# Two graph layers on one core: new order tables, fewer waits, and pair sums of the last group on GpSimd

## The reference

```python
def _L0_gnn_ref(item_embs, entity_embs, adj, W, a):
    scores = (Wh @ a1)[:, None] + (We @ a2)[None, :]
    e = jnp.where(scores > 0, scores, ALPHA * scores)      # ALPHA 0.2
    e = jnp.where(adj > 0, e, NEG_BIG)
    attention = jax.nn.softmax(e, axis=1)
    h_prime = attention @ entity_embs + item_embs
    return jax.nn.elu(h_prime)

def _L1_gnn_ref(x, adj_mat, U):
    deg = a.sum(axis=0)
    agg = jnp.einsum('ji,jd->id', a, x)
    return jax.nn.relu(agg @ U.T / deg[:, None])

h = jnp.maximum(_layernorm(x), 0.0)
x = x + _L0_gnn_ref(h, V, adj, W, a)
h = jnp.maximum(_layernorm(x), 0.0)
x = x + _L1_gnn_ref(h, adj, U)
```

## Time and profile before

| | us |
|---|---|
| median of 3 runs (415.91 to 420.17) | 417.25 |
| the profiled execution, its time | 417.24 |
| its span in the trace | 415.3 |
| PE busy | 347.2 (84%) |
| DVE busy | 298.0 (72%) |
| ACT busy | 275.2 (66%) |
| POOL busy | 115.0 (28%) |
| guards L828, 66 | 152.1 |
| scores L881, 41 | 49.3 |
| pair adds L890, 16 | 19.2 |

### The profile page before, as it was taken

One profiled execution on the slowest core, in us unless ns is written; L12 is line 12 of the kernel. 1 busy time (PEld: TensorE's weight loads), 2 busy tenths in 40 slices (PEclk: granted clock), 3 DMA queues, 4 the chain that ended last, 5 costly groups with the idle time before them and its releaser, 6 DMA issues.

```text
span 415.3 us, 17291 instructions
## 1 busy us (share of the span) xinstructions
PE 347.2 (84%) x7920; PEld 224.4 (54%) x7920; DVE 298.0 (72%) x423; ACT 275.2 (66%) x339; POOL 115.0 (28%) x120
## 2 busy tenths in 40 slices
PE   1737778298889797798899988899989899999996
PEld 0723555264456455454455434344534457999996
DVE  8799899457996568759984799965978683307333
ACT  2404789489998679779979999999788971110000
POOL 8674781784200460230050330020021010310000
PEclk9958999889999999989999999999999999999999
DMA  9999999999999999920000001000000000001100
GB/s 167 126 109 108 109 110 110 134 107 110 113 134 103 104 108 105 139 26 3 3 4 3 4 4 51 3 3 4 3 3 3 5 3 2 3 2 38 31 20 20
DMA packets 18727, 23.21 MB, mean 56 GB/s; under 512 B 13954, under 2 KB 14018, under 8 KB 18655
## 3 DMA queue, kind: packets, MB, share of 16 engines
q0 software_dynamic: 4752, 16.90, 39.1%
q1 hardware_dynamic: 11743, 4.65, 4.9%
q10 hardware_dynamic: 2160, 0.56, 0.7%
HBM read 71.71 MB, written 1.06 MB: 175 GB/s over the span
## 4 chain that ended last, share of the span: by engine, by line
PE 41%; ACT 21%; DVE 17%; issue 11%; DMA 5%; POOL 4%; SPq 0%; ACTq 0%; DVEq 0%; POOLq 0%
PE w L1202 10%; PE q L1319 10%; ACT arena L654 9%; PE q L1177 9%; DVE scratch L828 9%; ACT q L670 7%; PE den L1210 5%; PE w L1319 4%; DMA bi<-rows_sb 3%; DVE arena L881 3%; DMA adj_sb<-in_adj_dram 2%; DVE t_row L881 2%; ACT arena L658 2%; ACT t_row L658 1%; PE den L1319 1%
## 5 line engine op out<-in xcount | busy, mean ns | idle before, releaser
L828 DVE CUSTOM_DVE_ANT_0 scratch<-adj_sb,t_row 125x2048 uint8<-125x2048 uint8 x66 | 152.1, 2304 | 5.9 <-PE w L1249 1.2
L1202 PE MATMUL w<-arena,v_sb 128*32 128x500 f32 (+3 forms) x1144 | 132.8, 506 | 3.3 <-issue 3.3
L1177 PE MATMUL q<-bi,adj_sb 128*32 128x125 bf16 x4224 | 99.1, 222 | 37.2 <-ACT q L670 23.9
L1177 PEld LDWEIGHTS q<-bi,adj_sb 128*32 128x32 fp8e4 x4224 | 75.1, 97 | 84.2 <-ACT q L670 56.1
L654 ACT ACTIVATE arena<-q,t_col 128x1000 f32<-128x1000 f32 (+2 forms) x114 | 101.1, 890 | 8.3 <-PE q L1177 8.2
L1210 PE MATMUL den<-arena,ones 128*32 128x250 f32 (+1 forms) x960 | 82.2, 342 | 1.6 <-issue 1.6
L1210 PEld LDWEIGHTS den<-arena,ones 128*32 128x32 f32 x960 | 40.4, 110 | 50.9 <-issue 44.6
L670 ACT ACTIVATE q<-arena,minus_b 128x1000 f32<-128x1000 f32 (+1 forms) x65 | 55.6, 856 | 5.1
L670 ACT ACTIVATE q<-second_row,minus_b 128x750 f32<-128x750 f32 (+1 forms) x54 | 53.2, 985 | 8.0 <-DMA second_row<-s_dram 4.0
L1319 PE MATMUL q<-g_all,adj_sb 124*124 124x129 f16 (+2 forms) x693 | 41.2, 220 | 0.0
L1319 PEld LDWEIGHTS q<-g_all,adj_sb 124*124 124x124 fp8e4 (+2 forms) x693 | 40.8, 135 | 0.4 <-issue 0.4
(11 more groups left out here) (183 smaller groups left out, 348.7 us busy)
## 6 DMA issues: line engine op xcount, KB each, us to landing
adj_sb<-in_adj_dram POOLq DMA_DIRECT2D x33, 500.0 KB, 36.9
arena<-s_dram SPq DMA_DIRECT2D x2, 500.0 KB, 7.2
x_sb<-in_x_dram SPq DMA_DIRECT2D x1, 928.0 KB
out_dram<-x_sb SPq DMA_DIRECT2D x9, 84.0 KB
v_sb<-n_L_gnn_entity_embs_dram ACTq DMA_DIRECT2D x2, 256.0 KB, 5.6
v_sb<-n_L_gnn_entity_embs_dram SPq DMA_DIRECT2D x2, 256.0 KB, 4.8
second_row<-s_dram SPq DMA_DIRECT2D x1, 500.0 KB, 10.9
second_row<-s_dram SPq DMA_DIRECT2D x1, 375.0 KB, 10.1
```

The source lines that it names most:

```text
L828: nc.vector.tensor_tensor_reduce(out=junk[0:R, :], in0=adj_bytes[0:R, b, half], in1=t_row[0:R, half], scale=1.0 / ONE, scalar=0.0, op0=ALU ...
L1177: last = nc.tensor.matmul(q[n % Q_SLOTS][e:e + 32, bank, start:start + R], weights, bi[:, i % BI_SLOTS, k, :], start=not ON_ACT[n] and sta ...
L1202: last = nc.tensor.matmul(att(i)[h * D + d:h * D + d + 32, 0:(k1 - k0) * R], v_sb[:, c, d:d + 32], e[:, k0 * R:k1 * R], start=first, stop= ...
```

## The change

The numbers of `DVE_TILES`, `GUARD_TILES` and `WHEN` are new throughout. VectorE's tiles go from 2, 3, 9, 7 and 20 of the five groups to 2, 5, 10, 10 and 31. `wait_for_slot` is gone. The relu waits for the row in the first tile on ScalarE of each group only, and for the exp two tiles back only where that tile was ScalarE's too. In `guard` the wait for the block's DMA goes behind the wait for the guard before. `pair` goes from VectorE to GpSimd, where the four steps of the close of group 3 stand behind pairs 1, 5, 8 and 12; `close(4)` follows the last pair. The last group has eight slots of weights, the eighth in the row that group 3 has done with, and PE's `weigh_pair` comes one pair later.

```diff
-                 (0, 2, 4, 5, 6, 7, 8, 10, 13, 15, 17, 19, 20, 22, 24, 26, 27, 28, 30, 31)]
+                 (0, 1, 2, 3, 4, 5, 6, 7, 9, 10, 11, 12, 13, 14, 15, 16, 17, 18, 19, 20, 21, 22, 23, 24, 25, 26, 27, 28, 29, 30, 31)]
...
-        'range': (22, 28, 25, 27, None),
-        'turn_r': (28, 28, 28, 28, None),
-        'copy_r': (28, 28, 27, 28, None),
+        'range': (23, 26, 28, 24, None),
+        'turn_r': (27, 27, 28, 28, None),
+        'copy_r': (26, 26, 27, 27, None),
...
+    CLOSE_BEHIND = (1, 5, 8, 12)
     LAST = NI - 1
-    LAST_SLOTS, PAIRS = 7, NC // 2
+    LAST_SLOTS, PAIRS = 8, NC // 2
...
+            if i == LAST and c % LAST_SLOTS == LAST_SLOTS - 1:
+                return a_rows[(LAST + 1) % 2][:, 0:nb * R]
...
+            def pair(m):
+
+                n = NC * LAST + 2 * m
+                nb = GROUPS[LAST][1] - GROUPS[LAST][0]
+                pool.wait_ge(exped, n + 2)
+                pool.wait_ge(weighed, n + 1)
+                nc.gpsimd.tensor_tensor(e_slot(n, nb), e_slot(n, nb), e_slot(n + 1, nb), ALU.add).then_inc(paired, 1)
...
-            close(3)
-            close(4)
+            for m in range(PAIRS):
+                pair(m)
+                if m == CLOSE_BEHIND[0]:
+                    close_sum(LAST - 1)
+                if m == CLOSE_BEHIND[1]:
+                    close_centre(LAST - 1)
+                if m == CLOSE_BEHIND[2]:
+                    close_power(LAST - 1)
+                if m == CLOSE_BEHIND[3]:
+                    close_low(LAST - 1)
+            close(LAST)
...
                 if ON_ACT[n]:
-                    wait_for_slot(act, n)
                     act.wait_ge(masked, n + 1)
...
-                wait_for_row(act, i)
-                if n >= Q_SLOTS:
+
+                if n >= Q_SLOTS and ON_ACT[n - Q_SLOTS]:
                     act.wait_ge(exped, n - Q_SLOTS + 1)
                 if n < Q_SLOTS:
                     act.wait_ge(r1_ready, 1)
+                if c == min(k for k in range(NC) if k not in DVE_TILES[i]):
+                    wait_for_row(act, i)
...
-                if h == 0:
-                    dve.wait_ge(adj_in[b], 16)
                 for j in range(2, NI):
                     if (b, h) == (GROUPS[j][0], 0):
                         dve.wait_ge(natural, j - 1)
                 order = b * 2 + h
                 if order >= 1:
                     dve.wait_ge(guarded, order)
+                if h == 0:
+                    dve.wait_ge(adj_in[b], 16)
...
-                wait_for_slot(dve, n)
                 dve.wait_ge(masked, n + 1)
...
-            def pair(m):
...
-                if i == LAST and c >= 3 and c % 2 == 1:
-                    pair((c - 3) // 2)
...
-            pair(PAIRS - 1)
...
-                if i == LAST and c >= 5 and c % 2 == 1:
-                    weigh_pair((c - 5) // 2)
+                if i == LAST and c >= 7 and c % 2 == 1:
+                    weigh_pair((c - 7) // 2)
...
-            for m in range(PAIRS - 2, PAIRS):
+            for m in range(PAIRS - 3, PAIRS):
                 weigh_pair(m)
```

More of the change, by code:

```diff
@@ L67, in graph_layers_kernel @@
     WHEN = {
-        'copy_att': (None, 1, 1, 2, 5),
-        'copy_den': (None, 4, 1, 0, 0),
-        'natural': (None, 2, 2, 4, 7),
-        'normalise': (None, 8, 5, 4, 8),
-        'exp_hp': (None, 8, 7, 6, 9),
-        'elu': (None, 15, 9, 7, 10),
-        'elu_below': (None, 16, 10, 8, 11),
-        'square': (None, 9, 13, 10, 14),
-        'spread': (None, 16, 14, 15, 15),
-        'scale': (None, 20, 15, 17, 18),
-        'turn_h2': (None, 18, 20, 19, 20),
-        'copy_h2': (None, 18, 22, 21, 24),
@@ L92, in graph_layers_kernel @@
[L92 to L100 removed]
+        'copy_att': (None, 1, 1, 1, 2),
+        'copy_den': (None, 1, 2, 1, 1),
@@ new lines, in graph_layers_kernel @@
+        'natural': (None, 2, 1, 2, 6),
+        'normalise': (None, 3, 4, 2, 7),
+        'exp_hp': (None, 11, 6, 4, 13),
+        'elu': (None, 4, 9, 6, 9),
+        'elu_below': (None, 6, 9, 6, 15),
+        'square': (None, 16, 13, 10, 17),
+        'spread': (None, 12, 14, 12, 19),
+        'scale': (None, 18, 15, 14, 23),
+        'turn_h2': (None, 20, 18, 18, 24),
+        'copy_h2': (None, 21, 18, 25, 24),
+        'times_u': (None, 23, 20, 26, 25),
+        'high': (None, 25, 22, 27, 25),
@@ L482, in base, with close_sum @@
                     .then_inc(g_done, 1)
-            def close(i):
+            def close_sum(i):
                 b0, b1 = GROUPS[i]
-                nb = b1 - b0
                 pool.wait_ge(g_done, min(i + 2, NI))
@@ L501, in close, with close_low @@
                     .then_inc(rstd2_done, 1)
+            def close_low(i):
+                b0, b1 = GROUPS[i]
                 pool.wait_ge(rstd2_done, i + 1)
```

69 lines of the change are left out of this document (30 added, 39 removed), and 9 rows, old and new, of tables (DVE_TILES, GUARD_TILES).

## The result

The changed kernel takes 412.29 us (median of 5 runs, 411.94 to 413.76) against 417.21 for the kernel before (5 runs beside them, 415.91 to 420.17): a ratio of 0.9883, 95% interval 0.9844 to 0.9922. The profiled span is 410.1 us, 5.2 less than 415.3. I had forecast 404.2 and a range from 398.5 to 411.0. The direction was right; the gain is 4.9 us where 13.0 were forecast, and the time lies above the range.

A forecast was written before the change was run, and what follows sets the result against it. The prediction took ScalarE, VectorE and PE paces per tile, plus group borders, as the bounds. Savings in groups 0 to 4 less 1.0 us at the end made -13.0 us, from 417.25 to 404.2; range 398.5 to 411.

The forecast's parts named there:

- The waits: ScalarE's relus in groups 1 to 3: dropping the row wait saves 0.055 us each, together 3.9 us.
- Group 0: Exchanged waits in VectorE's six guards there, with the tile VectorE no longer has: 0.5 us gained, bounds 0 and 1.1.
- Group 1's end: Border to group 2: shifts ready earlier, tiles 27 to 31 run beside the DMA; 2.3 us gained, bounds 0 and 3.
- Group 2: Relu waits save 1.2 us and one more tile on VectorE saves 0.5.
- Group 3: Relu waits save 1.2 us and three more tiles on VectorE save 1.5.
- Group 4, the largest term: Last group, 31 tiles on VectorE, pair adds on GpSimd: first mask to last attend 54.5 us, gain 5.3, bounds 2 and 8.
- the rival of slow adds: GpSimd adds in group 4 take 3.2 us, not 2.3; the group gains 0.8, total 408.7 us; chance 0.10.
- the one where adds and tile passes exclude each other: In group 4 GpSimd adds and VectorE tile passes cannot overlap: 87 us there, total 436.5; chance 0.04.
- "three us": Group 4: five VectorE blocks of 0.6 to 1.6 us between tiles push later tiles back, about 3 us.
- The tail: After the last attend PE waits for GpSimd's last pair add; gather starts 1.0 us later, bounds 0.8 and 2.7.
- rivals each of which loses one stage: Guards delay VectorE's tiles in groups 2 and 3: 409.7 us, chance 0.14; ScalarE's waits were already hidden: 408.1, chance 0.10.
- "two of them together": Two of the first three rivals combine, leaving the time within 1%, 413.1 to 421.4 us; chance 0.06.

The follow-up runs named there:

- The waits alone: The kernel before with only the edits on waits, without new tables, slots or GpSimd adds: 412.34 us, ratio 0.9892.
- early wide masks: The changed kernel with masks made by matmuls of 128 columns, not 32, in groups 0, 1 and tiles 0 to 19 of group 2: 401.7 us.

## Why the prediction missed

Of 13.0 us forecast, 5.2 came in the span. Groups 1 and 2 fell short by 4.0 and 2.1 us, group 4 with its end by 3.3, group 3 by 0.1; group 0 gave 1.6 more than forecast.

**The bound of group 1 was misread.** The step that failed is the first: I took the stage windows and ScalarE's run as what sets group 1, and never asked what came next if ScalarE got faster. The trace of before held the answer. Waits of the kernel before in group 1:

```profile
PEld w L1202 <- issue: 4.2, 3, 1.9
```

Three gaps, up to 1.9 us long, with no releaser, in a stretch where the DMA share is 1.00. In their place the runs showed a block of 256 instructions each 6.0 us: more instructions lengthened the group by 11.2 us, fewer bytes beside them shortened it by 4.4, fewer instructions by 5.8. The Trainium skill describes the path: Runtime: NRT & Kernel Launch (Instruction fetch mechanics) says that TensorE's instructions come in 16 KiB blocks of 256 over a DMA queue of the sequencer's own, and calls the cost mostly hidden. The packets of queue 8 agree on the size. Here it was not hidden where the queues were full and PE could have used up a block in less than 6.0 us.

**The waits.** Right on the mechanism and the size: a hole of 0.03 and a period of 2.14, where I had 0.03 to 0.04 and 2.15. The waits alone gave 5.4 us of span where I had counted 3.9 for the relus; group 4's 12 relus, which I had left out, gave 1.1 of it, and 2.7 lie in groups 1 and 2, where the scatter is as large. I did not see that this was all that would be left.

**Group 0.** Forecast -0.5, measured -2.1, and not by what I had forecast: with the exchanged waits of the guards alone it was -0.1. The DMA that ends the group lasted 6.15 us (from 74.48) where it had been 7.67 (from 75.20). That 1.5 us is luck; why it was shorter was not tried.

**Group 1's end.** The shifts came earlier, as forecast: the last small operation of them began at 133.07 where it had been 137.08, 1.8 us earlier counted from the group's first mask, where I had 1.95 to 2.3. I had said that tiles 27 to 31 fit beside the DMA "by little", with the case that they take its place as the bound of 0. That bound is what happened. VectorE's timeline before group 2 in the changed kernel:

```profile
133.07 0.17 DVE L905 TENSOR_TENSOR halves<-neg_t,halves 125x8 bf16<-125x8 f32 x1
...
135.24 1.00 DVE L913 SCALAR_TENSOR_TENSOR arena<-second_row,b_col,q 128x750 f32<-128x750 f32 x1 [0.40 <-PE q L1204]
...
138.49 1.00 DVE L913 SCALAR_TENSOR_TENSOR arena<-second_row,b_col,q 128x750 f32<-128x750 f32 x1 [1.46 <-PE q L1204]
```

Tile 29's scores come 3.25 us after tile 28's, behind a gap named "issue" of 1.58 us on PE, in the middle of tile 29's mask, which goes on at 138.09. With early wide masks group 2 began at 137.08, right behind the DMA.

**Group 2.** Forecast -1.7, measured +0.4. Its first half is under the loads as well. With wide masks the change shortened it by only 0.6 (67.34 to 66.75), of which 0.4 are the waits; why it is not 1.7 there stays open.

**Group 3.** Forecast -2.7, measured -2.6, but not by my division. The waits alone gave 1.8. The tables took off another 0.8 and made VectorE the last, with one small operation held 0.87 us by GpSimd: the two terms were not independent, and that the sum fits is luck.

**Group 4, the largest term.** Forecast 54.5 us from the first mask to the last attend; measured 57.55, from 59.87. (The 11 us that I gave a pair are not the product of their terms: 6 tiles of 1.6 and 1.3 make 8.7. Nothing hung on it, since before the last add PE's weight loads waited for one 0.3 us at most, and its matmuls not at all.) The adds were sized right, 2.34 for 2.3, and the rival of slow adds (3.2) is out, as is the one where adds and tile passes exclude each other. The failed step is "three us" for VectorE's small blocks at the durations of before. I had excluded the waiting between the engines because group 4 has neither guards nor pair adds on VectorE. I looked at one direction, GpSimd waiting for a long VectorE instruction, and at the tile pass, which reads PSUM. The small operations over two SBUF inputs, and one over a single input, wait for GpSimd's 2.3 us instead, 4.9 us in all. The trace of before had a row of it too, in group 0: the same operation over 125x8 beside a GpSimd operation, and again where GpSimd had not begun:

```profile
48.91 0.90 DVE L743 TENSOR_SCALAR stat_a<-stat_a 125x8 f32<-125x8 f32 x1
```

```profile
48.85 0.93 POOL L464 TENSOR_TENSOR buf_b<-g_all,wa_row 125x384 f32<-125x384 f32 x1
```

```profile
77.72 0.17 DVE L743 TENSOR_SCALAR stat_a<-stat_a 125x8 f32<-125x8 f32 x1
```

With the variance moved, the last product later, the last add on VectorE and the adds in halves the same stretch took 53.6 us (last attend), below the forecast. GPSIMD Engine Reference (Specifications) of the Trainium skill names such contention for VectorE instructions of two SBUF inputs or in a 2-port mode, of which my prediction took up the first alone; the elu agrees, and L977 shows it for one input of 8 columns, whatever mode that ran in.

**The tail.** Forecast +1.0, measured +1.4.

**The chances.** I had given 0.14 and 0.10 to rivals each of which loses one stage. Two stages failed for reasons that had nothing to do with each other, and "two of them together" had only 0.06. The upper end, 411.0, stood on single failures.

## What to carry to other kernels

Before an engine's work is shortened, ask what stands right behind it in that stage: here another bound lay close by, and it was in the waits as a few long gaps named "issue" on PE while the DMA queues were full. Divide PE's instructions by 256 and the stage by that number; where the result equals the pace of other stretches under load, what helps is fewer instructions, even ones that are slower to run, or fewer bytes beside them. When GpSimd gets long operations, list each VectorE operation beside them that reads SBUF alone and is no reduction, and add the rest of a GpSimd instruction to it, or cut GpSimd's instructions short.
